# Reordering the loads of the first sample: half of the score operands and the late constants

## The reference, cut to what matters

```
x = _ln(src) * (1.0 + scale) + shift
q, k, v = projections of x, 16 heads of width 16
scores = einsum('bhqd,bhkd->bhqk', q / math.sqrt(HEAD_DIM), k) + attention_bias
probs  = softmax(where(src_mask, -inf, scores))
ctx    = einsum('bhqk,bhkd->bhqd', probs, v)
x = x + (ctx @ Wo + bo)
h = _ln(x) * g2 + beta2
ff = _gelu2(h @ W1 + b1) @ W2 + b2
```

## Time and profile before

| | |
|---|---|
| median of 3 runs | 982.52 us (981.4 to 982.77) |
| the profiled execution | 980.44 us |
| its span, first to last instruction | 978.6 us |
| mean granted TensorE clock | 0.994 of full |
| PE busy | 926.8 us, 95% of the span |
| DVE, POOL, ACT busy | 75%, 72%, 68% |
| first sample's attention | about 34 to 118 us of the span |

### The profile page before, as it was taken

How to read it: one execution, slowest core, us unless ns; L and a number is a source line. 1 busy time by engine, 2 the same in 40 slices (tenths; PEclk the granted TensorE clock), 3 DMA queues, 4 the chain that set the end, 5 groups by cost and what they waited for, 6 DMA issues and landing times. The chain is left out here.

```text
span 978.6 us, 19957 instructions
## 1 busy us (share of the span) xinstructions
PE 926.8 (95%) x5758; PEld 614.0 (63%) x5838; DVE 737.4 (75%) x1991; ACT 670.3 (68%) x1118; POOL 708.5 (72%) x568
## 2 busy tenths in 40 slices
PE   5889999999999999999999999979899999999996
PEld 5656556656656655665665665545476777777574
DVE  8886887878879788788986978788345675668465
ACT  3576978898788787889878878878544453544333
POOL 1789789788878878978896897876454455558465
PEclk9999999999999999999999999999999999999998
DMA  8988988996997899799789889965211110111101
GB/s 301 337 312 280 375 326 273 341 392 228 329 390 288 288 379 349 247 341 390 248 310 391 291 290 373 367 228 172 84 44 44 44 44 24 42 66 44 44 22 65
DMA packets 127533, 229.96 MB, mean 235 GB/s; under 512 B 6512, under 2 KB 53872, under 8 KB 123632
## 3 DMA queue, kind: packets, MB, share of 16 engines
q1 hardware_dynamic: 127472, 229.26, 65.8%
HBM read 187.30 MB, written 41.94 MB: 234 GB/s over the span
## 5 line engine op out<-in xcount | busy, mean ns | idle before, releaser
L937 ACT ACTIVATE prob<-prob,nmax 128x512 f32<-128x512 f32 x512 | 357.9, 729 | 65.7 <-DVE nmax L760 62.5
L760 DVE CUSTOM_DVE_ANT_0 prob<-s_bank,big 128x512 f32<-128x512 f32 x512 | 339.0, 686 | 74.0 <-POOL big L1111 39.0
L591 PEld LDWEIGHTS t_bank<-ident,prob 128*128 128x128 f32 x2048 | 239.0, 141 | 163.7 <-issue 48.2
L591 PE MATMUL t_bank<-ident,prob 128*128 128x128 f32 x2048 | 317.0, 277 | 16.1 <-ACT prob L937 6.0
L1111 POOL TENSOR_TENSOR big<-big,mterm_early 128x2048 f32<-128x2048 f32 (+2 forms) x78 | 271.0, 3489 | 50.2 <-DMA big<-in_fside_Bx16xSxS 34.1
L944 ACT COPY pt<-t_bank 128x512 f32<-128x512 f32 x312 | 182.0, 587 | 42.4 <-PE t_bank L591 41.2
L579 PE MATMUL s_bank<-stack_k,stack_q 128*128 128x512 bf16 x432 | 165.1, 382 | 1.3 <-DVE nmax L760 0.7
L769 DVE COPY pt<-t_bank 128x512 f32<-128x512 f32 x200 | 137.5, 688 | 31.3 <-PE t_bank L591 30.9
L605 PE MATMUL o_bank<-pt,val 128*32 128x512 f32 x1024 | 123.2, 599 | 3.7 <-issue 1.0
L2209 POOL TENSOR_TENSOR gl<-big,gh 128x512 fp32r<-128x512 f32 x64 | 83.1, 1307 | 49.8 <-DVE gh L1751 49.8
L2060 ACT ACTIVATE big<-bank,late 128x512 f32<-128x512 f32 x62 | 42.6, 690 | 72.6 <-PE bank L1458 69.8
(11 more groups left out here) (248 smaller groups left out, 1460.4 us busy)
## 6 DMA issues: line engine op xcount, KB each, us to landing
big<-in_fside_Bx16xSxS SPq DMA_DIRECT2D x128, 1024.0 KB, 7.7
pieces_dram<-pieces SPq DMA_DIRECT2D x64, 384.0 KB, 6.9
stack_q<-pieces_dram SPq DMA_DIRECT2D x15, 1024.0 KB, 8.8
stack_k<-pieces_dram SPq DMA_DIRECT2D x15, 1024.0 KB, 9.9
pieces_dram<-pieces SPq DMA_DIRECT2D x32, 256.0 KB, 7.2
xin<-in_x SPq DMA_DIRECT2D x8, 512.0 KB, 8.7
x_dram<-x SPq DMA_DIRECT2D x8, 512.0 KB, 4.5
x1r<-x_dram SPq DMA_DIRECT2D x8, 512.0 KB, 4.6
```

Source lines behind the costliest of these rows:

```text
L591: last = pe.transpose(t_bank[n % 2][:, c * P:(c + 1) * P], prob[:, n % NT, c * P:(c + 1) * P], ident[:])
L760: dve.tensor_tensor_reduce(out=prob[:, n % NT, :], in0=s_bank[n % 3][:, :], in1=bias[:, h % NB, t, :], scale=-1.0, scalar=3e38, op0=ALU.ad ...
L937: act.activation(tile, tile, ACT.Exp, bias=nmax[:, n % NT:n % NT + 1], scale=-1.0).then_inc(exped.sem, 1)
```

## The change

In the first sample the q and k stacks of the second half are issued after heads 4 and 5, where they were issued after heads 0 and 1. The late constants are issued after head 9, where they were issued after head 3. Later samples keep their order. Within a head SP's order is: bias, late constants, expert, mask, piece stores, first half's stacks, second half's stacks.

```diff
-HEADS_OF_LOADS = dict(x1=3, first=2, expert=4, W1=6, mask=5, store_0=7, store_1=11)
-STACK_0_AT, STACK_1_AT = (9, 10), (0, 1)
+HEADS_OF_LOADS = dict(late=9, x1=3, first=2, expert=4, W1=6, mask=5, store_0=7, store_1=11)
+STACK_0_AT, STACK_1_AT, STACK_1_FIRST = (9, 10), (0, 1), (4, 5)
...
-                    if h == HEADS_OF_LOADS["x1"] and first:
+                    if h == HEADS_OF_LOADS["late"] and first:
                         sp.dma_start(k["late"][:], d["late"]).then_inc(k["late_in"], 16)
...
-                    if h in STACK_1_AT:
-                        load_stack(b - 1, 1, STACK_1_AT.index(h), first=first)
+                    if first and h in STACK_1_FIRST:
+                        load_stack(b - 1, 1, STACK_1_FIRST.index(h), first=True)
+                    if not first and h in STACK_1_AT:
+                        load_stack(b - 1, 1, STACK_1_AT.index(h))
```

## The result

The changed kernel takes 983.53 us (median of 22 runs, 980.19 to 987.66) against 981.17 us for the kernel before on the same chips: ratio 1.0025, interval 1.0015 to 1.0035. It is slower by about 2.4 us, where no change was forecast. (The time itself, 983.53 us, lies only 1.0 us above the forecast of 982.5 us. That is partly luck: the forecast stood on a median of 3 runs, 982.52 us, and 22 runs of the same kernel give 981.17 us.) Two more timings of it beside other variants gave 1.0013 (0.9999 to 1.0026) and 1.0011 (0.9998 to 1.0024). The profiled execution took 987.30 us, 3.8 us over its median; 4.2 us of its excess over the profile before arise in and behind the last sample, and no other profile of the changed kernel shows them.

A forecast was written before the change was run, and what follows sets the result against it. POOL was taken to bound heads 4 to 9 of the first sample. The terms −1.65 + 1.33 + 0.53 − 0.16 gave +0.05 us, so the median stays at 982.5 us, range 979.7 to 984.5.

The forecast's parts named there:

- The lead: POOL's bias waits at heads 5 and 6 go, putting it 2.44 us earlier; PE gains 1.65 us.
- PE's four waits at 83 to 92 us: Short PE waits of 0.32, 0.30, 0.26 and 0.77 us, 1.65 together, forecast to go if POOL is early.
- The step that failed: Between 54 and 82 us PE and DVE were said not to follow POOL, so nothing is won there.
- The list of what would show it: Signs expected in the profile after, among them PE's 2.27 us wait unchanged and a new k stack wait near 1.3 us.
- five rivals: On time 0.20, undamped 0.15, clock 0.15, late stack 0.10, and the change not doing what it says, no share.
- The k stack: Scores of step 32: the stack lands at 76.15, stalling PE by +1.33 us, bounds 0 and 3.0.
- The late constants: 652 KB after head 9 delay later biases in the full queue: +0.53 us, bounds 0.53 and 1.65.
- the dip of the earlier trace: From 98.5 to 100.5 us the queue ran at 185 GB/s against 419, taken to absorb 1.12 us.
- Head 15: The sample's end follows the landing of head 15's bias; slack of 0.16 us, counted as −0.16.
- The clock rival: Head 4's bias lands up to 1 us sooner and the 1.2 GHz fall, 1.7 us, goes: 979.8 us; chance 0.15.
- The late stack rival: The k stack takes 10.4 us, PE stalls 3.0 at step 32, clock falls for 1.7: 985.9 us; chance 0.10.
- The on-time rival: The k stack lands by 74.85 without a stall: −1.3 us, 981.2 us; chance 0.20.
- The undamped rival: No queue dip absorbs the late constants, which cost 1.65 us: +1.2 us, 983.7 us; chance 0.15.

The follow-up runs named there:

- e9: The changed kernel with ACT in place of DVE normalising x in the first sample, one step earlier; 981.00 us, 1.0008 of the kernel before.
- e2: The kernel before with only the late constants moved behind head 9, the stacks as before; 981.33 us, 1.0003 of the kernel before.
- e11: The kernel before with ACT normalising x in the first sample and nothing else changed; 981.23 us, 1.0001 of the kernel before.
- e3: The changed kernel, but in the first sample POOL begins head 5's mask only when DVE has normalised x; 982.08 us, 1.0005 of the kernel before.
- e4: The kernel before with four unread additions on POOL behind head 4's mask, no load moved; only profiled, one execution of 980.54 us.
- e1: The kernel before with only the stacks moved, after heads 4 and 5, the late constants left after head 3; 981.46 us, 1.0002 of the kernel before.
- e14: The same kernel as e3, run a second time; 982.94 us, 1.0007 of the kernel before.
- e7: The changed kernel with POOL waiting as in e3 and the late constants after head 8 in place of 9; 980.41 us, 0.9990 of the kernel before.
- e15: The same kernel as e7, run a second time; 980.78 us, 0.9986 of the kernel before.
- e5: The changed kernel without an edit, run again beside other variants; 982.46 us.
- e13: The changed kernel without an edit, run a third time; 983.10 us.
- e6: The kernel before with 16 unread matmuls on PE ahead of its wait for the normalised x in the first sample; 981.69 us, 1.0000 of the kernel before.
- e10: e9 with the stacks after heads 3 and 4 and the late constants after head 8; 980.11 us, 0.9991 of the kernel before.
- e12: The changed kernel with the stacks after heads 3 and 4 in place of 4 and 5; 982.45 us, 1.0014 of the kernel before.
- e16: The same kernel as e4, now timed; 983.25 us, 1.0005 of the kernel before.

## Why the prediction was wrong

**The lead.** "POOL is 1.81 + 0.63 = 2.44 us earlier from there on": right in its cause, 2.03 us at head 9, of 3.09 us at head 7, by its own rows. PE's four waits at 83 to 92 us are gone, and PE is busy for all of 80 to 90. In the changed kernel PE also came over 2 us late to them, which would close them too; that the lead does it is shown by e9, where PE is on time and they are gone. But their size was that of one profile: in e2, the same kernel up to head 9, they sum to 0.99 us, and in e11 to 0.67, where the forecast had 1.65.

**The step that failed** is the costing of that lead between 54 and 82 us: "so nothing is won there". Nothing was won, but the possibility that something is lost was not priced. The text took POOL's waits of 1.81 and 0.63 us for pure loss. The first was the room in which DVE normalised x. With it filled, the four instructions cost 2.7 us more, and PE's wait 2.2 us more. That is more than the 1.65 us that the lead was to give. Nor was the premise quite right that DVE does not follow POOL there: at 58.90 us in the profile before DVE had waited 0.54 us for POOL. PE also ran 6.82 us at the 1.2 GHz level in 50 to 70 us, in place of 3.42, but that is not shown to come of the stretch: e2 and e3 have 6.8 us with the normalising at 1.38 us, and e4 has 3.42 with it at 4.32. The list of what would show it said that PE's 2.27 us wait would still be there; it was 4.43. None of the five rivals had this in it, though the row of the four instructions and POOL's idle row stood side by side in the timeline.

**The k stack.** Forecast +1.33 us within 0 and 3.0. Measured in the changed kernel 1.12, 0.5 and none, with 1.4 us in e1. That the first is near the forecast is luck. The load was issued at 69.14 us in place of 67.45 and landed at about 78.1 in place of 76.15, since the late DVE also held back the bias of head 9 (68.08 us, where it was 66.31), behind which the load stands. PE, held by the same instructions, came to step 32 at 77.05 us in place of 74.82. Two errors of about 2 us cancel. The assumed latency of 8.7 us was fair (9.0, 8.5 and 7.8 in the three). Where the normalising is undisturbed and the stacks go out after heads 4 and 5, the stall is none, 0.27, 0.64 and 1.45 us (e3, e14, e7, e15). The estimate by the Trainium skill's page SBUF — State Buffer, section The DMA setup-cost knee, no stall, was too small for two of the three.

**The late constants.** Forecast +0.53 us within 0.53 and 1.65. In the profile after, the dip of the earlier trace rows is filled, as assumed:

```profile
98.50:100.50 2.00, 2.00 (x15) 1.36 (x14) 1.89 (x7) 2.00 (x5) 2.00 (x2) 1.00 1.04 423
```

and head 12 to head 15 takes 12.94 us, 0.43 more than before. In the other two profiles of the changed kernel it takes 13.67 and 11.00 us (e5, e13); in all three, head 12 itself begins late by different amounts, so this time says little. But where PE is on time it takes 1.15 us more (e2), and 1.0 us of that is given back by moving them one head forward (e3 and e14 against e7 and e15). There the term of 0.53 us was about half of what it measured.

**Head 15.** That the slack is short (0.16 us) was read rightly: DVE waits there now, 0.88 us for the mask of head 15 (timeline of DVE after):

```profile
115.94 0.69 DVE L762 CUSTOM_DVE_ANT_0 prob<-s_bank,big 128x512 f32<-128x512 f32 x1 [0.88 <-POOL big L1110]
```

**The clock rival** fell: head 4's bias took 8.6 us to land in both kernels, so the queue keeps its order, and e6 shows no gain from a whole clock while POOL bounds. **The late stack rival** did not happen: no profile has a stall near 3 us. **The on-time rival** had the stack right in one of the three profiles of the changed kernel, but its end was wrong all the same, since the stretched normalising cost more than the gain, and e10, without stretch and stall, shows no gain from the lead up to head 12 either. **The undamped rival** comes nearest in time, 983.7 us, but its shift is +1.2 us where +2.4 was measured, and its 1.65 us for the late constants are more than any profile shows.

**What stays open.** In the profiles the stretched normalising and its cause are shown. To the second record the change costs 1.9 to 2.3 us, of which POOL's wait gives back 1.0 to 1.6 and the late constants one head earlier another 1.0 to 1.2. In time, three timings of the changed kernel (1.0025, 1.0013, 1.0011), two with POOL's wait (1.0005, 1.0007) and two with the late constants also moved (0.9990, 0.9986) stand in the order that the profiles give, and the two ends differ clearly. How the 2.4 us divide between stretch, late constants, stall and half clock can't be told from the times: each step is about as large as an interval, and of the kernels with the stretch e12 was slower beyond its interval and e1 and e16 were not.

## What to carry to other kernels

Before a wait of POOL is removed, look at what DVE does in it: an in-place fp32 operation on SBUF may be living in that gap, and its cost triples when POOL runs on. Read the idle time of one engine as possible cover for another, not as loss alone. And when a load is moved, move it to where the queue is seen idle; here one head made 1 us. Compare two profiles from an event that the edit can't have moved, since an earlier chance difference of 1 to 2 us looks like a gain.

## What the runs showed of the hardware

An in-place DVE `tensor_scalar` of 128x256 fp32 in SBUF took 0.41 us with POOL silent and 1.24 us with POOL adding tiles back to back, with the DMA queue full (e4) as with it half empty (after). ACT's form of the same tile, 2.07 us for four, ran beside a busy POOL. PE's time at the 1.2 GHz level in 50 to 70 us did not follow the length of its wait for the normalised x. It was 3.42 us in the profile before (wait 2.3 us) and 6.82 in e2 (1.4), 6.83 in e3 (2.1) and 3.42 in e14 (2.4), which are one kernel, 3.42 in e4 (4.1), none in e7 (1.2) and 10.24 in e16 (5.3).
